# Mixture-of-experts feed-forward: the second expert matrix as three f16 products on router-weighted activations, eight experts summed transposed in one PSUM bank

## What is computed

```python
x = L0_attn_x
x = x + 0.5 * ffn(layernorm(x), Wr, W1, W2)
x = x + attention(layernorm(x), qkv_w, qkv_b, out_w, out_b)
x = x + 0.5 * ffn(layernorm(x), Wr, W1, W2)

# ffn, with E = 8 experts, F = 256, K = 2
logits = flat @ Wr.T
weights, ids = top_k(logits, K); weights = softmax(weights)
h = einsum('nc,efc->nef', flat, W1)
val, gate = h[..., :F], h[..., F:]
act = val * silu(gate)
expert_outputs = einsum('nef,ecf->nec', act, W2)
out = einsum('nec,ne->nc', expert_outputs, router_weights)
```

## Time and profile before

| | |
|---|---|
| median of 3 runs | 1325.09 us (1322.58 to 1326.47) |
| the profiled execution | 1324.05 us, of it a span of 1322.1 us from the first to the last instruction |
| granted TensorE clock, mean | 0.984 of full speed |
| PE busy | 1269.0 us (96%), 10240 matmuls |
| DVE busy | 1112.9 us (84%) |
| ACT busy | 809.9 us (61%) |
| POOL busy | 143.4 us (11%) |
| first feed-forward | from the start to about 354 us |
| attention | to about 1010 us |
| second feed-forward | to the end |

### The profile page before, as it was taken

The page is one execution under the profiler, slowest core; times in us unless marked ns, Lnnn a source line. Parts: engine busy times, 40 slices in busy tenths (PEclk is TensorE's granted clock), DMA queues, the critical chain, the costliest instruction groups (busy, mean ns, idle before and its releaser), DMA issues.

```text
span 1322.1 us, 32042 instructions
## 1 busy us (share of the span) xinstructions
PE 1269.0 (96%) x10240; PEld 616.0 (47%) x10240; DVE 1112.9 (84%) x2306; ACT 809.9 (61%) x1540; POOL 143.4 (11%) x450
## 2 busy tenths in 40 slices
PE   6999999999889999999999999999999999999998
PEld 3666666667522222222222222222223776767776
DVE  7888867887789999999999999999994787777775
ACT  4433333333239999999999999999997333333332
POOL 1020122111221111111111111111110000000000
PEclk9999999999969999999999999999998999999999
DMA  7010111011211100101101011010010100000000
GB/s 207 1 30 19 49 49 48 12 37 49 67 54 32 42 31 31 40 30 39 32 30 40 31 31 40 30 40 31 31 54 14 35 27 27 27 27 21 13 9 9
DMA packets 52265, 48.49 MB, mean 37 GB/s; under 512 B 10080, under 2 KB 44768, under 8 KB 52192
## 3 DMA queue, kind: packets, MB, share of 16 engines
q1 hardware_dynamic: 52192, 47.61, 12.4%
HBM read 23.86 MB, written 23.33 MB: 36 GB/s over the span
## 4 chain that ended last, share of the span: by engine, by line
PE 89%; DVE 5%; issue 4%; ACT 1%; DVEq 0%; DMA 0%; ACTq 0%; SPq 0%
PE ps L765 23%; PE ps L906 22%; PE ps L893 21%; PE ps L752 16%; PE ps L722 2%; PE ps L864 1%; PE ps L742 1%; DVE X L1092 1%; PE ps L686 1%; PE ps L883 1%; PE ps L729 1%; ACT probs L661 1%; DVE mx L1235 1%; DVE act L1080 1%; PE ps L759 1%
## 5 line engine op out<-in xcount | busy, mean ns | idle before, releaser
L1235 DVE TENSOR_REDUCE mx<-ps 128x1 f32<-128x1024 f32 x512 | 591.7, 1217 | 35.9 <-PE ps L864 30.0
L661 ACT ACTIVATE probs<-ps 128x512 f32<-128x512 f32 x1024 | 562.4, 597 | 60.7 <-PE ps L893 42.6
L590 ACT ACTIVATE sg<-ps,unscale 128x512 f32<-128x512 f32 x256 | 173.8, 687 | 307.2 <-PE ps L765 283.0
L906 PE MATMUL ps<-probs,vh 128*32 128x256 f32 x4096 | 330.7, 395 | 16.9 <-issue 11.5
L893 PE MATMUL ps<-Q,K 51*128 51x512 bf16 x1024 | 333.3, 386 | 0.9 <-ACT probs L661 0.5
L864 PE MATMUL ps<-K,Q 48*128 48x512 bf16 x1008 | 327.1, 389 | 2.9 <-DVE mx L1235 2.5
L752 PEld LDWEIGHTS ps<-w,act 128*128 128x128 f32 x2048 | 247.9, 192 | 17.1
L752 PE MATMUL ps<-w,act 128*128 128x128 f32 x2048 | 249.0, 275 | 0.0
L1080 DVE SCALAR_TENSOR_TENSOR act<-ps,unscale,sg 128x512 f32<-128x512 f32 x256 | 183.3, 744 | 60.0 <-ACT sg L590 19.2
L765 PE MATMUL ps<-x_hi,w_hi 128*128 128x512 f16 x512 | 195.6, 382 | 9.9 <-DVE act L1080 6.4
L1092 DVE SCALAR_TENSOR_TENSOR X<-ps,rw,X 128x128 f32<-128x128 f32 (+1 forms) x512 | 143.9, 343 | 62.4 <-PE ps L752 61.8
(11 more groups left out here) (84 smaller groups left out, 608.9 us busy)
## 6 DMA issues: line engine op xcount, KB each, us to landing
o_parts<-ot SPq DMA_DIRECT2D x64, 128.0 KB, 1.9
q_stack<-parts SPq DMA_DIRECT2D x48, 128.0 KB, 2.3
k_stack<-parts SPq DMA_DIRECT2D x48, 128.0 KB, 2.3
Q<-q_stack SPq DMA_DIRECT2D x64, 96.0 KB, 2.3
K<-k_stack SPq DMA_DIRECT2D x64, 96.0 KB, 2.3
probs<-w_in SPq DMA_DIRECT2D x8, 256.0 KB, 4.3
att<-o_parts SPq DMA_DIRECT2D x16, 128.0 KB, 2.6
rden<-rdens SPq DMA_DIRECT2D x16, 128.0 KB, 2.5
```

The costliest lines, as they stand in the source:

```text
L590: nc.scalar.activation(sg[:, j, :], hid[2 * j], ACT.Silu, scale=unscale[:, e, 2 + j:3 + j]).then_inc(silu_done, 1)
L661: nc.scalar.activation(probs[:, kb % PSLOTS, j * CH:(j + 1) * CH], score[i], ACT.Exp, scale=SCALE).then_inc(probs_ready, 1)
L906: last = nc.tensor.matmul(opsum[VW * c:VW * (c + 1), :], vh[:, u % 2, kb, :], probs[:, kb % PSLOTS, c * QW:(c + 1) * QW], start=(kb == 0), ...
L1235: nc.vector.tensor_reduce(mx[:, u % 2, t:t + 1], pair.rearrange("p a b -> p (a b)"), AX_X, ALU.max).then_inc(max_read, 1)
```

## The change

Chunk 0 of each feed-forward stays as it was (f32 `expert_out`, `accumulate`). For chunks 1 to 7 (`mixed_chunk`):

- `gated` multiplies with `gate_scale` in place of `unscale`.
- GpSimd's new `weigh` multiplies `act` in place with the router weight of each token, spread over all partitions (`rwb`): one 128x512 f32 instruction for each e and j.
- ScalarE's new `act_hi_part` copies the product to f16, VectorE's new `act_lo_part` subtracts that copy from it (two SBUF inputs, f16 result).
- TensorE's new `mix_out` makes six f16 matmuls of 512 columns for each expert, with the weights `w2_hi`, `w2_lo` stationary. All eight experts add up in one bank, features by tokens. It runs two experts behind the hidden products.
- Once in a chunk: `mix_copy` (ScalarE, PSUM to SBUF with a scale), `mix_back` (four transposes on TensorE) and `add_mix` (VectorE, one 128x512 addition into `X`). They replace the eight `accumulate`.
- The router weights go through `rw_transpose` (TensorE), `rw_t_copy` (ScalarE), a store to memory and two broadcast loads (`spread_weights` on SP, 2 MB for a chunk) into the memory of `probs`.
- Once in the run: `w2_scales`, `mix_power`, `mix_scales` and the small `top_transpose`, `top_spread` find a power-of-two scale; `w2_hi_part` (ScalarE) and `w2_lo_part` (VectorE, 16 instructions of 128x128 with two SBUF inputs) split W2 in chunk 1 of the first feed-forward.
- `add_bias` moves from VectorE (four 128x128) to GpSimd (one 128x512). The split of q and k moves to chunk c - 2, a piece at a time between the `weigh` instructions. Moments, routing and the attention's pieces are placed at other experts, mostly earlier. VectorE's hardware loop makes one round, the rest is written out.

```diff
-                    if not (first and e == 0):
-                        expert_out(m - 1, (e - 1) % E)
+            def mix_out(f, c, e):
+                pe.wait_ge(act_lo_ready, 2 * mix_step(f, c, e) + 2)
...
+                for j in range(2):
+                    for i, (w, x) in enumerate(((w2_hi, act_hi), (w2_hi, act_lo), (w2_lo, act_hi))):
+                        last = nc.tensor.matmul(mixpsum, w[:, e, j, :], x[f][:, e % 2, j, :],
...
+            def weigh(f, c, k, e):
...
+                for j in range(2):
+                    pool.wait_ge(act_ready, 2 * m + j + 1)
+                    nc.gpsimd.tensor_tensor(act[:, e % 2, j, :], act[:, e % 2, j, :], rwb[k][:, e, :],
+                                            ALU.mult).then_inc(act_weighed, 1)
...
+            def act_hi_part(f, c, e, j):
+                n = mix_step(f, c, e)
+                sc.wait_ge(act_weighed, 2 * n + j + 1)
...
+                nc.scalar.activation(act_hi[f][:, e % 2, j, :], act[:, e % 2, j, :], ACT.Copy).then_inc(act_hi_ready, 1)
...
+            def act_lo_part(f, c, e, j):
+                n = mix_step(f, c, e)
+                dve.wait_ge(act_hi_ready, 2 * n + j + 1)
...
+                nc.vector.tensor_tensor(act_lo[f][:, e % 2, j, :], act[:, e % 2, j, :], act_hi[f][:, e % 2, j, :],
+                                        ALU.subtract).then_inc(act_lo_ready, 1)
...
+            def add_mix(f, c):
+                dve.wait_ge(back_in_psum, mixed(f, c))
+                alone(dve)
+                xs = X[:, bass.ds(c * TPC, TPC), :].rearrange("p t d -> p (t d)")
+                nc.vector.tensor_tensor(xs, backpsum, xs, ALU.add).then_inc(y_added, 1)
```

ScalarE's `mixed_chunk`, with the places of the pieces of the split of q and k:

```diff
+                for e in range(E):
+                    if e == 2 and not second:
+                        mix_copy(f, c - 1)
+                    for j in range(2):
+                        silu(p, e, j)
+                        if e > 0:
+                            act_hi_part(f, c, e - 1, j)
+                        elif not second:
+                            act_hi_part(f, c - 1, E - 1, j)
...
+                    if f == 0:
+                        if not second:
+                            if e == 0:
+                                mid_part(c - 2, 0)
+                            if e == 1:
+                                hi_part(c - 2, 1)
+                            if e == 2:
+                                mid_part(c - 2, 1)
+                        if e == 5:
+                            x2T_copy(c - 1)
+                        if e == 7:
+                            hi_part(c - 1, 0)
```

More of the change, by code:

```diff
@@ L373, in _ @@
             load_head(0, 2)
-            store_parts(NCH // CPB - 1, 1)
+            for u in range(CPB):
+                store_parts(NCH - CPB + u, NCH // CPB - 1, u)
             load_mrow(0, 0)
@@ new lines, in ffn @@
+            def ffn(f):
+                mixed_chunk(f, 1, 1, second=True)
+                with pool.Fori(1, NCH // CPB - 1) as r:
+                    for u in range(CPB):
+                        mixed_chunk(f, CPB * r + u, u)
+                mixed_chunk(f, NCH - 2, 0)
+                mixed_chunk(f, NCH - 1, 1)
+            pool.wait_ge(w_loaded, 16 * 7)
+            ffn(0)
+            qk_rest(NCH - 2, 0)
+            qk_sum(NCH - 2, 1)
+            qk_lo(NCH - 2, 0)
+            qk_rest(NCH - 2, 1)
@@ L491, in _ @@
+            qk_lo(NCH - 2, 1)
+            add_bias(NCH - 1)
+            for w in range(2):
+                qk_sum(NCH - 1, w)
+                qk_rest(NCH - 1, w)
+                qk_lo(NCH - 1, w)
             PER = 4
@@ L606, in ffn_chunk @@
[L606 to L616 removed]
+                    if e == 2 + f:
+                        xT_copy(p + 1, 1)
@@ L617, in ffn @@
+            def ffn(f):
+                first_chunk(f)
+                mixed_chunk(f, 1, 1, second=True)
                 with sc.Fori(1, NCH // CPB - 1) as r:
                     for u in range(CPB):
-                        chunk(CPB * r + u, u)
-                chunk(NCH - 2, 0)
-                chunk(NCH - 1, 1, more=False)
+                        mixed_chunk(f, CPB * r + u, u)
+                mixed_chunk(f, NCH - 2, 0)
+                mixed_chunk(f, NCH - 1, 1, more=False)
+                for j in range(2):
+                    act_hi_part(f, NCH - 1, E - 1, j)
+                if f == 0:
+                    mid_part(NCH - 2, 0)
+                    hi_part(NCH - 2, 1)
+                mix_copy(f, NCH - 1)
+                if f == 0:
+                    mid_part(NCH - 2, 1)
@@ new lines, in first_chunk, with mixed_chunk @@
+                    if e == 7:
+                        if f == 1:
+                            pe.wait_ge(add_order, 3)
+                        rw_transpose(f, 1, 1, tpsum)
+            def mixed_chunk(f, c, k, second=False, more=True, proj=True):
+                p = NCH * f + c
+                for e in range(E):
+                    if e == 0:
+                        pe.wait_ge(x_lo_ready, p + 1)
+                    for j in range(2):
+                        gate(p, e, j, k)
+                        value(p, e, j, k)
+                        if j == 0 and e == 2 and not second:
+                            mix_back(f, c - 1)
+                        if j == 0 and e == 6 and f == 0:
+                            q_or_k(c - 1, 0)
+                    if more:
+                        if e == 1:
+                            x_transposes(p + 1, 1 - k, 0 if second or f else c - 1)
+                        if e == 2:
+                            router(p + 1, 1 - k, 0 if second or f else c - 1)
+                        if e == 5:
+                            rw_transpose(f, c + 1, 1 - k)
+                    if f == 0:
+                        if e == 0 and not second:
+                            values(c - 2)
+                        if e == 0 and second:
+                            top_spread()
+                        if e == 5:
+                            x2_transposes(c - 1)
+                        if e == 7:
+                            q_or_k(c - 1, 1)
+                    elif e == 5 and proj:
+                        out_projection(c + 2)
+                    if e > 1:
+                        mix_out(f, c, e - 2)
+                    elif not second:
+                        mix_out(f, c - 1, E - 2 + e)
+                    elif e == 0:
+                        expert_out(f, E - 1)
@@ L812, in ffn @@
+            def ffn(f):
+                if f == 0:
                     w_transposes(0)
-                    x_transposes(p0, 0, 0)
-                    router(p0, 0, 0)
-                chunk(0, 0, first=True, loads=not attended)
-                if not attended:
+                    x_transposes(0, 0, 0)
+                    router(0, 0, 0)
+                first_chunk(f)
+                if f == 0:
                     pe.wait_ge(w_loaded, 16 * 7)
-                chunk(1, 1)
+                mixed_chunk(f, 1, 1, second=True)
@@ new lines, in mixed_chunk @@
+                    for j in range(2):
+                        gated(f, c, e, j)
+                        if e > 0:
+                            act_lo_part(f, c, e - 1, j)
+                        elif not second:
+                            act_lo_part(f, c - 1, E - 1, j)
+                        elif j == 0:
+                            accumulate(f, E - 1)
+                        if j == 0 and e == 2 and not second:
+                            add_mix(f, c - 1)
+                    if f == 0 and second:
+                        if e == 0:
+                            mix_scales()
+                        else:
+                            w2_lo_part(e - 1)
+                            if e == E - 1:
+                                w2_lo_part(e)
```

612 lines of the change are left out of this document (426 added, 186 removed).

## The result

The changed kernel takes **1454.07 us** (median of 4 runs, 1452.84 to 1455.62) against 1324.63 us (1322.58 to 1326.47) for the kernel before: a ratio of 1.098, with a 95% interval of 1.096 to 1.100. It is 129 us slower, where +24 was forecast and 1400 was the top of the range.

The account below looks back on a forecast made before the run. TensorE bounded the kernel; VectorE with its port waits would bound most chunks after the change. Terms 25 + 3 + 4.5 - 9 + 3.5 - 3 = +24 us on 1324.05 gave 1349 us, 8-in-10 range 1292 to 1400.

Parts of the forecast that it names:

- the likeliest case: Whole kernel: VectorE's line with the port wait sets the time, slower, 1325 to 1390 us; chance 0.50, 0.46 of it slower.
- TensorE's need: TensorE per chunk: net 3.4 us saved, needing 37.7 us in the first and 33.7 in the second feed-forward.
- VectorE's busy time without the port: VectorE per chunk: 34.5 us in the first and 30.4 in the second feed-forward, with some 1 us of own waits.
- The port: VectorE's two-SBUF-input instructions wait for GpSimd: 4.7 us a chunk at `act_lo`, plus 0.6 for `norm_attention` in the second feed-forward.
- VectorE's line sets the chunk: Second feed-forward: VectorE's busy time plus waits, 36.7 us, is the chunk's length, against 37.13 before; seven chunks sum to -9.
- The first feed-forward: Chunks take 45 us against 41.1 to 41.9: +3.6 each for chunks 2 to 5, together +25 with the others.
- ScalarE's three waits for the split: First feed-forward: ScalarE waits for GpSimd's pieces of q and k, 1 us each, 3 us a chunk; bounds 0 and 3 x 2.5.
- Setup and ends: Chunk 0's scale setup +3, the end of the first feed-forward +4.5, the end of the run +3.5 us.
- the forecast's -3 for the loops' turns: VectorE's loop turns no more, the others' do: half of some 3 us in the first feed-forward and the second's excess, -3.
- GpSimd takes the port twice: Rival: a waiting `weigh` goes before a longer-waiting `act_lo`, 9 us more a chunk, 1464 us; chance 0.06.
- TensorE stays the bound: Rival: VectorE's spare time covers the waits, so TensorE's saving shows: 1298 us, at best 1288; chance 0.32.
- The clock rival: A TensorE that waits drops to granted clock 0.69; with half the chunks affected about 1420 us; chance 0.05.

Follow-up runs that it names:

- e5: Changed kernel with GpSimd's product with the router weights replaced by a write-only fill of a scratch tile about as long: 1396.7 us, ratio 1.055.
- e7: Changed kernel without GpSimd's weighing (semaphore only) and with the second feed-forward's once-a-chunk steps at other experts: 1330.4 us, ratio 1.004.
- e12: Changed kernel without GpSimd's weighing, second feed-forward's once-a-chunk steps moved, and the split of q and k later in the first: 1321.4 us, ratio 0.997.
- e3: Changed kernel, full computation, both feed-forwards: norm, routing and transposes one expert later, `norm_attention` three experts earlier: 1419.2 us, ratio 1.072.
- e2: Changed kernel in which GpSimd only passes the semaphore on and multiplies nothing (router weights left out): 1350.6 us, ratio 1.020.
- e4: Changed kernel, full computation, with the pieces of the split of q and k one or two experts later on ScalarE and GpSimd: 1436.3 us, ratio 1.085.
- e8: Changed kernel, full computation, with once-a-chunk steps moved in both feed-forwards and the split of q and k later: 1396.9 us, ratio 1.056.

## Why the prediction was wrong

- **Sign and port right, size far off.** Slower, by VectorE's wait at the port, was the likeliest case; +24 was said and +129 came. The wait is there (e5), but by itself `weigh` makes the smaller part: 5.0 of the 12.8 us in a chunk of the second feed-forward (below).
- **TensorE's need: right.** 33.7 us computed, 33.76 measured (e7). In the first feed-forward 37.7, measured 38.2 (e12).
- **VectorE's busy time without the port: right.** 30.4 and 34.5 us computed; 30.04 (e7) and 35.2 (e12; 36.2 in e7, where the pieces of the split stand earlier).
- **The port: near for act_lo, missed for the one-input instructions.** In e3 the mean durations, from the listing by line, are 884 ns for `act_lo` against 682 without `weigh`: 16 x 0.20 = 3.2 us, where I took 4.7. `norm_attention` has 1754 against 690: 1.1 us, where I took 0.6. `wt` and `var` have 1.23 against 0.16, `xn` 0.57 against 0.34: 2 x 1.07 + 4 x 0.23 = 3.1 us, which I had at 0, having excluded one-input instructions by the rotate and tile maximum of the earlier trace rows, which read PSUM. Sum 7.4, forecast 5.3; e3's busy time less e7's is 7.5. In the trace of the kernel before no TENSOR_SCALAR out of SBUF meets a GpSimd instruction in the feed-forwards: `var` and `wt` take 0.17 us at most there, `xn` 0.35. It could not show their wait, nor rule it out.
- **The step that failed: "VectorE's line sets the chunk".** I added up what VectorE does and took the sum (36.7 us) for the chunk, as though a bound engine never idled. TensorE's waits at `attn`, `xn` and `rw` stand in the sum with nothing; they are 24 us in three chunks (13.3, 6.4 and 4.3). VectorE can run ahead by one expert only, and TensorE's queue is in order: a late `attn` or `xn` stops the hidden products behind it, and VectorE then starves. The four corners of the second feed-forward show the size, each the mean of the last five distances:

| chunk, us | steps where the change put them | steps moved |
|---|---|---|
| without `weigh` | 37.7 (e2) | 33.9 (e7) |
| with `weigh` | 46.7 (after) | 38.9 (e3) |

  `weigh` alone costs 5.0 us, the places alone 3.8, both together 12.8. The slower VectorE makes the misplaced steps later: TensorE's longest wait for `attn` is 4.4 us, and 2.3 in e2. TensorE's clock falls behind the longer waits: the granted clock over these chunks is 0.91, and 0.99 in e2. How much of the 4.0 us beyond the sum is the clock's was not told apart.
- **The first feed-forward: mis-sized.** 1 us was taken for each of ScalarE's three waits for the split, with 2.5 as the upper bound. They are up to 4.9 us long, 60.4 us in the stretch from 128 to 380 us (five chunks); moving the split later gave back 2.7 us a chunk (e4). With the split and the places moved 46 us remain, of which e8's VectorE is busy 44.4 of 46.5; with `weigh` left out too, 41.0 (e12).
- **Setup and ends.** The end of the run took 8.1 us from the last `gated` to the store, in place of 4.6: 8 was forecast. Chunk 0 of the second feed-forward was not in the sum at all.

The sum's terms beside the spans of the two traces (the forecast's -3 for the loops' turns belongs to no one row):

| stretch | forecast | measured |
|---|---|---|
| first feed-forward, chunk 0 | +3 | +1.9 |
| chunk 1 | +9 | +12.0 |
| chunks 2 to 6 | +16 | +39.0 |
| chunk 7, to the first product of queries and keys | +4.5 | +13.6 |
| from there to the second feed-forward's first hidden product | 0 | -0.1 |
| second feed-forward, chunk 0 | 0 | +15.7 |
| chunks 1 to 7 and the end | -5.5 | +48.0 |

From the end of the changed kernel, the timeline of all engines:

```profile
1441.42 0.75 DVE L1396 SCALAR_TENSOR_TENSOR act<-ps,gate_scale,sg 128x512 f32<-128x512 f32 x1
...
1449.49 0.40 SPq L517 DMA_DIRECT2D out<-X  x1
```

- **The rivals.** "GpSimd takes the port twice" gave 1464, close to the result, by a mechanism that did not occur: the mean of `act_lo` is 0.87 to 0.90 us, not 1.9. A number that fits proves nothing about its cause. "TensorE stays the bound" is what e7 shows, with the router weights left out, for the second feed-forward only. The clock rival was right in kind: the waits here are 2 to 5 us, beyond the 2 us I had set against it, and the windows have a granted clock of 0.88 to 0.93 (the rival took 0.69).

What stays open: how much of e5's remaining chunk time is the small waits and how much the longer chain; whether chunk 0 of the second feed-forward comes back to 35 us with its attention steps at other experts; and a version in which GpSimd multiplies `sg` before `gated`, with the result kept in PSUM so that `act_lo` has one SBUF input, which was not tried.

## What to carry to other kernels

Before adding up an engine's busy time as the length of a stage, look at each once-a-stage step in the other engines' in-order queues: how late may it be, what stands behind it, and by how many buffers can its producer run ahead. Here lateness from contention and badly placed steps cost more together (12.8 us a chunk) than apart (5.0 and 3.8), so test the placement with the contention removed and with it in place. GpSimd is not free parallel capacity beside a VectorE with little slack: count VectorE's instructions with two SBUF inputs, and those with SBUF alone on both sides even if they are tiny.
